# Graph layers and expert block on one core: the last phase's hi and lo rows transposed by DMA

## The reference, cut to what matters

```python
for l in range(3):
    h_neigh = segment_sum(h[src], dst) / deg
    rst = relu(h @ W_self[l] + h_neigh @ W_neigh[l] + b[l])
    h = rst / maximum(norm(rst), EPS)
x = x + h
xn = layer_norm(layer_norm(x), ln_g, ln_b)
logits = xn @ Wg                       # 8 experts
h = gelu(xn @ W1 + b1)                 # 8 x 64 hidden
o = h @ W2 + b2
x = x + layer_norm(layer_norm(x) + sum_of_top_2(o, conf), out_g, out_b)
```

## Time and profile before

| | before |
|---|---|
| median of 3 runs | 2274.31 us (2273.78 to 2278.62) |
| the profiled execution, its own time | 2276.38 us |
| its span in the profile | 2274.7 us |
| mean granted TensorE clock | 0.965 |
| busy: PE / DVE / POOL / ACT | 2088.6 / 1773.4 / 1253.7 / 991.2 us |
| DMA moved | 343.48 MB, mean 151 GB/s |

### The profile page before, as it was taken

One profiled execution on the slowest core, in us unless ns is written; L12 is line 12 of the kernel. 1 busy time (PEld: TensorE's weight loads), 2 busy tenths in 40 slices (PEclk: granted clock), 3 DMA queues, 4 the chain that ended last, 5 costly groups with the idle time before them and its releaser, 6 DMA issues.

```text
span 2274.7 us, 45187 instructions
## 1 busy us (share of the span) xinstructions
PE 2088.6 (92%) x15941; PEld 1178.0 (52%) x15947; DVE 1773.4 (78%) x4201; ACT 991.2 (44%) x1698; POOL 1253.7 (55%) x1396
## 2 busy tenths in 40 slices
PE   1989899888799999998899999996499999999997
PEld 0444444344344444444444444443277777777775
DVE  4778997556588888886788888885589999999974
ACT  1232212111344433432334443343677777777751
POOL 4771003771465665664444444444578888888744
PEclk9999999999899999999899999998599999999998
DMA  4553345883455555554566666665445565556533
GB/s 129 143 152 125 114 133 132 112 113 113 127 174 176 171 174 175 172 175 139 190 216 215 223 212 218 219 215 168 135 115 133 133 140 134 133 131 135 139 44 41
DMA packets 162789, 343.48 MB, mean 151 GB/s; under 512 B 32153, under 2 KB 32327, under 8 KB 162567
## 3 DMA queue, kind: packets, MB, share of 16 engines
q0 software_dynamic: 60816, 165.43, 28.0%
q1 hardware_dynamic: 101751, 175.16, 26.3%
HBM read 175.81 MB, written 165.31 MB: 150 GB/s over the span
## 4 chain that ended last, share of the span: by engine, by line
PE 77%; POOL 8%; DVE 6%; issue 6%; ACT 2%; DMA 1%; SPq 0%; DVEq 0%; POOLq 0%; ACTq 0%
PE psS L486 30%; PE psY L486 22%; PE psY L1699 9%; POOL slot_table L633 4%; PE psT L1616 4%; PE psA L1656 2%; PE psA L1657 2%; POOL node_info L633 2%; PE psS L1723 2%; PE psT L1671 1%; PE psA L486 1%; PE psY L1709 1%; PE psY L1701 1%; PE psA L1733 1%; POOL scl L656 1%
## 5 line engine op out<-in xcount | busy, mean ns | idle before, releaser
L486 PE MATMUL psY<-w_n,HT 128*128 128x512 f16 x2844 | 671.0, 387 | 46.6 <-DVE HT L1202 44.8
L486 PE MATMUL psS<-w_s,HT 128*128 128x512 f16 x2844 | 652.5, 379 | 0.0
L486 PEld LDWEIGHTS psY<-w_n,HT 128*128 128x128 f16 x2844 | 279.6, 99 | 402.4 <-DVE HT L1202 60.0
L486 PEld LDWEIGHTS psS<-w_s,HT 128*128 128x128 f16 x2844 | 268.4, 98 | 280.4
L868 ACT ACTIVATE RR<-R 128x512 f32<-128x512 f32 x237 | 149.4, 631 | 286.8 <-DVE R L1325 281.4
L735 POOL DMA_INDIRECT y_rows<-YB,poutT x158 | 160.9, 1019 | 188.7 <-DVE YB L1209 160.4
L728 POOL TENSOR_TENSOR scl<-ssm,halfpow 128x1 f32<-128x1 f32 x158 | 88.8, 562 | 246.9 <-DVE ssm L1343 246.9
L486 PE MATMUL psS<-w_w,raw 128*128 128x512 f16 x948 | 217.5, 379 | 0.0
L832 ACT ACTIVATE HH<-R 128x512 f16<-128x512 f32 x79 | 49.7, 628 | 364.8 <-DVE R L1187 330.7
L1202 DVE COPY HT<-psT 128x1024 f16<-128x1024 f16 x237 | 162.2, 685 | 41.3 <-PE psT L1616 39.8
L1219 DVE SCALAR_TENSOR_TENSOR SB<-psS,downs,bias 128x512 f32<-128x512 f32 x237 | 177.9, 751 | 10.6 <-PE psS L486 9.7
(11 more groups left out here) (280 smaller groups left out, 3713.3 us busy)
## 6 DMA issues: line engine op xcount, KB each, us to landing
self_rows<-SB SPq DMA_DIRECT2D x236, 256.0 KB
Sl<-self_rows SPq DMA_DIRECT2D x158, 256.0 KB
X<-in_x_dram SPq DMA_DIRECT2D x78, 256.0 KB
y_rows<-YB SPq DMA_DIRECT2D x78, 256.0 KB
out_dram<-obb SPq DMA_DIRECT2D x78, 256.0 KB
raw<-in_L_gnn_W_neigh_dram SPq DMA_DIRECT2D x12, 256.0 KB
raw<-in_L_gnn_W_self_dram SPq DMA_DIRECT2D x12, 256.0 KB
y_rows<-YB,poutT POOLq DMA_INDIRECT x158, 3.0
```

Source lines behind the costliest of these rows:

```text
L486: mm = eng.matmul(acc, lhs[:, a, c, :], w[:, bpart, c, :], start=(n == 0), stop=(stop and n == 3 * KC - 1))
```

## The change

The PE stage `turn_x` and the ACT stage `txc` go. SP gets a stage `turn_x` at offset -1, behind `load_self3`: when both halves of tile s-1 are in `HH`, it issues one transposing DMA from `HH[i]`, seen as 128 x 1024, into the ring buffer of `HTR`, seen as 128 x 8 x 128. Every ring slot has its own semaphore `f3.ht[q]`. `gate` waits for it in place of `txc`, and `xhi` waits for the DMA of two tiles before, as it overwrites what that one reads.

```diff
-FFN_RING = 8
+HT_RING = 8
...
+            def turn_x(t):
+                t = t.own
+                i, q = t.slot(2), t.slot(HT_RING)
+                sp.wait_ge(f3.xhi, (t + 1).n)
+                sp.wait_ge(f3.xlo, (t + 1).n)
+                after(sp, f3.down, (t + (1 - HT_RING)).n)
+                to = HTR[q]
+                sp.dma_start_transpose(to.rearrange("p a c n -> p (a c) n"), HH[i].rearrange("p a n -> p (a n)")
+                                       ).then_inc(f3.ht[q], 16)
+
+            run_tiles(T, [(6, load_self3), (-1, turn_x)], 2)
...
                 act.wait_ge(f3.xn, (t + 1).n)
-                after(act, f3.tx, (t + -1).n)
+                if t.t >= 2:
+                    act.wait_ge(f3.ht[(t + -2).slot(HT_RING)], (t + -2).landed(HT_RING))
                 act.activation(HH[i][:, 0, :], XN[i], ACT.Copy).then_inc(f3.xhi, 1)
-
-            def txc(t):
-                t = t.own
-                act.wait_ge(f3.tx, (t + 1).n)
-                after(act, f3.down, (t + (1 - FFN_RING)).n)
-                act.activation(HTR[t.slot(FFN_RING)], psX[:, :, :, :], ACT.Copy).then_inc(f3.txc, 1)
...
-            run_tiles(T, [(4, lambda t: carry_hi(t, 3)), (-2, txc), (-8, fhi), (4, lambda t: relu(t, 3)),
+            run_tiles(T, [(4, lambda t: carry_hi(t, 3)), (-8, fhi), (4, lambda t: relu(t, 3)),
...
-            def turn_x(t):
-                t = t.own
-                i = t.slot(2)
-                pe.wait_ge(f3.xhi, (t + 1).n)
-                pe.wait_ge(f3.xlo, (t + 1).n)
-                after(pe, f3.txc, t.t)
-                for a in range(2):
-                    for c in range(KC):
-                        mm = pe.transpose(psX[:, a, c, :], HH[i][:, a, c * P:(c + 1) * P], iden16[:, :])
-                mm.then_inc(f3.tx, 1)
-
             def gate(t):
                 t = t.own
-                pe.wait_ge(f3.txc, (t + 1).n)
+                pe.wait_ge(f3.ht[t.slot(HT_RING)], t.landed(HT_RING))
                 after(pe, f3.logit, t.t)
...
-            run_tiles(T, [(4, lambda t: aggregate(t, 3)), (-2, turn_x), (-9, down), (4, carry_rest), (-7, turn_w),
+            run_tiles(T, [(4, lambda t: aggregate(t, 3)), (-9, down), (4, carry_rest), (-7, turn_w),
                           (-7, up), (-7, spread_w), (-2, gate)], 2)
```

More of the change, by code:

```diff
@@ L198, in __init__ @@
         self.xlo = sem("f3_xlo")
-        self.tx = sem("f3_tx")
-        self.txc = sem("f3_txc")
+        self.ht = [sem(f"f3_ht{i}") for i in range(HT_RING)]
         self.gate = sem("f3_gate")
@@ L473, in build @@
         st6b = sb("st6b", [P, 6])
-        psX = psT[0]
         psWT = psT[1].rearrange("p a c n -> p (a c n)")
@@ L590, in load_self3 @@
                 sp.dma_start(Sl[t.slot(2)][:, :], Sd[2][bass.ds(t.t * P, P), :]).then_inc(s.xs[t.slot(2)], 16)
-            run_tiles(T, [(6, load_self3)], 2)
+            def turn_x(t):
[8 more added lines that the diff above has]
+            run_tiles(T, [(6, load_self3), (-1, turn_x)], 2)
         @block.gpsimd
@@ L1661, in _ @@
                                      (0, lambda t, l=l: own(t, l)), (3, lambda t, l=l: aggregate(t, l))], l - 1)
-            def turn_x(t):
-                t = t.own
-                i = t.slot(2)
-                pe.wait_ge(f3.xhi, (t + 1).n)
-                pe.wait_ge(f3.xlo, (t + 1).n)
-                after(pe, f3.txc, t.t)
-                for a in range(2):
-                    for c in range(KC):
-                        mm = pe.transpose(psX[:, a, c, :], HH[i][:, a, c * P:(c + 1) * P], iden16[:, :])
-                mm.then_inc(f3.tx, 1)
             def gate(t):
                 t = t.own
-                pe.wait_ge(f3.txc, (t + 1).n)
+                pe.wait_ge(f3.ht[t.slot(HT_RING)], t.landed(HT_RING))
                 after(pe, f3.logit, t.t)
-                products(pe, psG[:, 0:EXPERTS], HTR[t.slot(FFN_RING)], wg16.rearrange("p c (a e) -> p a c e", a=2)
+                products(pe, psG[:, 0:EXPERTS], HTR[t.slot(HT_RING)], wg16.rearrange("p c (a e) -> p a c e", a=2)
                          ).then_inc(f3.gate, 1)
@@ L1690, in up @@
                 t = t.own
-                h = HTR[t.slot(FFN_RING)]
+                h = HTR[t.slot(HT_RING)]
                 w = WT["w1"]
```

## The result

| | before | after |
|---|---|---|
| median, same chip | 2274.05 us (2273.56 to 2278.62, 4 runs) | 2248.95 us (2248.52 to 2250.78, 4 runs) |
| ratio | | 0.9883 [0.9867, 0.9899] |
| span of the profiled execution | 2274.7 us | 2246.8 us |
| mean granted TensorE clock | 0.965 | 0.967 |

What follows compares the result with a forecast made beforehand. PE was taken to bound the kernel at 7.90 us a step; steps of 9.4 us gave +97.5 us steady, +21.6 at the start, -3 at the end, together +116: 2390 us, range 2255 to 2575.

Steps and rivals of the forecast that it cites:

- the loop: Once a step: gate, aggregate, carry, combine to R, SP's load, transpose, next gate; a turn takes 2.4 us + L.
- The price of the transposes: On PE, eight transposes between aggregate and `down` take 0.45 us in each of 79 steps, which the change removes.
- PE's step of 7.45 us: PE's need per steady step without transposes if nothing new waited, down from 7.90, above DVE's 7.21.
- the rival: The wait at gate vanishes as A + T is under 5.05 us: -29 us steady, about 2250 us; chance 12%.
- ACT's copies: One ACT copy of 1.00 us a step goes, saving no time by itself: ACT is busy 6.11 of 7.90 us.
- L: Time from the issue of the load of `Sl` to the landing of the transpose behind it, taken as 7.0 us.
- the sum 71 x p - 551: Whole change in us, p being the time of a step, taken as 9.4 us; about +116 us.
- break-even at p = 7.76: Step time at which the change neither gains nor loses, equal to A + T = 5.4 us.
- The smaller risk: PE idling 2 us of 9.4 could lower its granted clock; a fall costs up to 0.73 us a step in the loop.
- A and T: Parts of L on SP's queue: A, the load ahead, 4.4 us; T, the transpose itself, 2.6 us.
- my dearer bounds: Sizes for the transposing DMA itself: 2.6 us taken, 6.0 by engine time per piece, 12.6 by packet start pace.

Runs made afterwards that it cites:

- e1: The changed kernel with the load of `Sl` waiting for the next tile's R, the transpose issued behind it: 2385.65 us, ratio 1.047 to the kernel before.
- the second experiment: The changed kernel with transpose and load of `Sl` both waiting for the next tile's R, transpose issued first: median 2382.91 us, executions 2321.9 to 2426.29.

## Why the prediction was wrong, point by point

**The step that failed** is the place of the transpose in SP's order ("in step s SP first waits for R of tile s+5"). `after(sp, s.r, (t + -1).n)` waits for the count of tile t-1, and a count of n means that tiles up to n-1 are done: the load of tile s+6 waits for R of tile s+4. The section on the kernel before, ahead of the prediction, says "once R of tile s+5 is there"; that is wrong, too. With the right tile DVE's own order gives the rest. R of s+4 and `xlo` of s-1 lie in the same step of DVE, `xlo` last, so SP finds R first, sends the load, waits for `xlo`, and sends the transpose long before the next R. The transpose hangs on no R and no load, the loop isn't closed, and the gate has 6.8 us.

The trace of before held the answer. The last load of `Sl` is that of tile 78, the last tile; these are SP's issues and DVE's R at the end of the phase, by their lines and by the timeline of the kernel before:

```profile
L590 SPq DMA_DIRECT2D Sl<-self_rows x3: 319/320/320, 2141.2 to 2157.0; - x3
...
2156.29 0.73 DVE L1325 SCALAR_TENSOR_TENSOR R<-psA,invs,Sl 128x512 f32<-128x512 f32 x1
...
2164.44 0.73 DVE L1325 SCALAR_TENSOR_TENSOR R<-psA,invs,Sl 128x512 f32<-128x512 f32 x1
2171.99 0.73 DVE L1325 SCALAR_TENSOR_TENSOR R<-psA,invs,Sl 128x512 f32<-128x512 f32 x1
```

Two R follow the one that released it, those of tiles 77 and 78: the load of 78 went out at R of 76. In the earlier trace rows I had paired the load at 1904.47 with the `xlo` at 1901.63, and the right partner is the `xlo` after it. A count of instructions from the end of the phase would have told.

**The price of the transposes** on PE: 0.45 us a step by the earlier trace rows, and right: 7.83 to 7.38 in two of four steps, 7.87 to 7.38 in a third. What was wrong was to take it for every step: the fourth took 8.04 us in before and takes 8.04 in after.

**PE's step of 7.45 us, with DVE at 7.21 just behind:** the average became 7.545, as DVE's group step of 8.04 stayed, 0.165 us a step above 7.38. I compared the mean busy times of the engines only; the steps of DVE aren't alike, and the long one decides. So the steady steps gave 23 us and not the rival's 29, and the start, for which it had allowed up to 8 us more, gave 0.9 instead; its 2250 fits to a microsecond, better than its terms do. Nor do these terms give its range: -29, -3 and up to +8 from 2274.3 make 2242 to 2250, not 2246 to 2258.

**ACT's copies** "save no time by themselves": right as far as the runs tell (one transpose on PE, all copies: 7.44 us in two of four steps, as the PE work alone gives).

**The loop of 2.4 us + L, the sum 71 x p - 551, break-even at p = 7.76:** the loop was right in e1, 2.51 us in the turn shown. The sum gave 109 us where the span grew by 97: its term for the start was too large, 21 us for 8.6, as steps taken at 9.9 took 6.8 to 8.4.

**The smaller risk**, the clock: it came with the closed loop and cost more than the 0.73 us set for a fall. A step with the fall in it took 9.07 us in place of 7.38, 13 times at most in e1.

**A and T:** L as a whole was 7.13 us in that turn and 9.29 - 2.51 = 6.8 on average (the clock's part included), for 7.0. Its split was wrong. Without the load ahead the forecast's terms give 2.4 + 2.6 = 5.0 us, no wait at all; the run gave 8.54 a step. T isn't one number: 3.0 us from issue to landing in a quiet stretch, up to 8.7 beside gathers and outputs. The reason that the closed loop so often met the bad end, as I read it, is that R stands at the time when POOL sends the next gather (1899.04 and 1899.08); in after the transpose goes out 4 us later. The load's own duration in the earlier trace rows may have come from the same traffic; no run took that apart.

The rule that on each DMA engine a queue's descriptors are consumed in ring order (the Trainium skill, "DMA: Bandwidth & Descriptors", "Queues, rings and completion order") isn't contradicted; it only had nothing to act on in after, where but seven packets of the load are left when the transpose is issued.

The other page of the Trainium skill that was cited, "Advanced Engine Details and Errata" ("X-Bar Transpose (TRN2)"), says that transposing DMAs are as fast as regular ones. In the quiet window 0.26 MB in 1.5 us is nearer to that than to any of my dearer bounds (0.90 us by bytes alone, 2.6 taken, 6.0 and 12.6 as upper ends). Beside POOL's transfers it took far longer, but so did the plain load in before, 3.7 to 4.9 us to its last packets; no run has both in the same place, so the comparison stays open there.

The 1309 ns for a block of 128 x 128 of the Trainium skill's "VectorE: DVE Perf Modes" ("The three transpose paths") don't add up over blocks: in the quiet case eight of them in one DMA landed 3.0 us after the issue, that issue included.

**The chances:** I gave the rival 12%, and its condition was A + T under 5.05 us. It came true by another way: the wait wasn't where I had put it. A rival "the transpose doesn't stand behind R at all" was missing from the list, and a wrong reading of one index had 82% on the wrong side.

**Left open:** which of the gathers, the outputs, `X` and the instruction queue's packets stretches a transpose by how much, and by what mechanism (58 and 48 instead of 21 ns a packet); why the kernel without gathers still takes 8.03 us a step where its landings are 3.3 us in the median (late R on DVE and the outputs both have a part, not measured apart); and what makes the executions of the second experiment differ by 104 us beyond the clock's part.

## What to carry to other kernels

Before a moved step is priced, settle which tile's event releases it, and do it by counting instructions in the trace from one end of the phase, not from the index arithmetic alone: one tile here is the difference between -25 and +105 us. A transfer that was issued early cost no step here, even at twice the traffic; tied to an event of the current step it costs what its landing takes, here 3.0 to 8.7 us, so look at what other queues send at the same moment. A wait on the critical path can cost twice, as the clock fell after it here. When the bounding engine becomes faster, look at the longest step of the next one, not at its mean, and reorder its stages so that what the bounding engine waits for comes first.

## What the runs showed of the hardware

- A transposing DMA of 128 x 1024 float16 is 1056 packets, 1024 of 256 bytes. Alone they took 21 ns of an engine each and 1.5 us in all, with 3.0 to 3.1 us from issue to landing; the plain packets of the same queue average 94 ns. Small packets were not dear.
- The issue occupies SP's queue for 1.24 us against 0.32 us for the load of `Sl`. In after nothing that is waited for stood behind it.
- Beside GpSimd's indexed transfers the same transpose took up to 8.7 us to land, at 58 ns a packet (71 in the first half) near a gather and an output, and at 48 ns near an output alone.
- After a step in which PE idled 4.3 of 11.9 us the granted clock fell for part of the next: mean 0.81, and 9.07 us for PE work of 7.38.
- The DMA share of a stretch can read 1.05 with no step longer than at 0.60. A high share alone was no sign of a bound.
